# Row maxima of the scores in four row tiles of 32 rows, one group of four per key tile step

## The reference, cut to what matters

```
qh, kh, vh = proj(layernorm(x), Wq, bq), proj(ctx, Wk, bk), proj(ctx, Wv, bv)
scores = einsum('bhqd,bhkd->bhqk', qh, kh) / sqrt(16)
attn   = softmax(scores, axis=-1)          # over the 1601 keys
out    = einsum('bhqk,bhkd->bhqd', attn, vh) @ Wo.T + bo
```

## Time and profile before

| | |
|---|---|
| median of 3 runs | 684.64 us (683.98 to 685.73) |
| the profiled execution | 684.26 us, of which the profile's span is 682.4 us |
| prologue (first batch's keys and maxima) | 0 to 41 us |
| attention, 8 batches, 7 of them with units of the next | 41 to 470 us, the last batch from about 436 us |
| experts | 470 us to the end |
| busy: TensorE, VectorE, ScalarE, GpSimd | 655.0, 473.3, 326.9, 296.1 us |
| TensorE clock granted | 90% of full speed or more in all 40 slices |

### The profile page before, as it was taken

How to read it: one execution, slowest core, us unless ns; L and a number is a source line. 1 busy time by engine, 2 the same in 40 slices (tenths; PEclk the granted TensorE clock), 3 DMA queues, 4 the chain that set the end, 5 groups by cost and what they waited for, 6 DMA issues and landing times.

```text
span 682.4 us, 16188 instructions
## 1 busy us (share of the span) xinstructions
PE 655.0 (96%) x6618; PEld 538.7 (79%) x6626; DVE 473.3 (69%) x870; ACT 326.9 (48%) x533; POOL 296.1 (43%) x386
## 2 busy tenths in 40 slices
PE   7989999999999989999999999979999999999996
PEld 4778878878867867877887787656788999999996
DVE  4887757667657688584977857479778666666653
ACT  4355655554454554455446453446555444444431
POOL 1137797896676688675668766400000000000000
PEclk9999999999999999999999999999999999999999
DMA  5311110100010010011001000062003203320000
GB/s 164 144 49 51 28 48 26 49 26 26 26 35 16 26 50 25 26 34 41 9 20 48 1 2 1 2 248 88 37 1 124 103 22 124 123 109 14 0 0 31
DMA packets 12853, 34.12 MB, mean 50 GB/s; under 512 B 1515, under 2 KB 9972, under 8 KB 10612
## 3 DMA queue, kind: packets, MB, share of 16 engines
q1 hardware_dynamic: 12756, 33.19, 14.6%
q0 software_dynamic: 32, 0.01, 0.0%
HBM read 32.67 MB, written 0.52 MB: 49 GB/s over the span
## 4 chain that ended last, share of the span: by engine, by line
PE 81%; DVE 9%; issue 5%; ACT 2%; POOL 2%; DMA 0%; POOLq 0%; DVEq 0%; ACTq 0%
PE bank L1154 45%; PE bank L1340 13%; PE bank L1163 9%; PE bank L1224 5%; POOL prob_sum L481 2%; PE bank L1264 2%; PE bank L1273 2%; DVE prob_sum L481 1%; DVE ctx_lo L465 1%; DVE maxes L877 1%; ACT probs L719 1%; ACT k_hi L615 1%; PE bank L1248 1%; DVE k_lo L858 1%; PE bank L1370 1%
## 5 line engine op out<-in xcount | busy, mean ns | idle before, releaser
L481 POOL TENSOR_TENSOR prob_sum<-probs,prob_sum 128x256 f32<-128x256 f32 x336 | 266.3, 824 | 80.6 <-ACT probs L719 76.3
L719 ACT ACTIVATE probs<-bank 128x1024 f32<-128x1024 f32 (+1 forms) x104 | 106.6, 1025 | 122.9 <-PE bank L1340 107.9
L877 DVE TENSOR_REDUCE maxes<-bank 128x1 f32<-128x400 f32 (+1 forms) x256 | 131.3, 566 | 21.6 <-PE bank L1224 19.7
L701 ACT ACTIVATE h_raw<-bank,b_sb 128x512 f32<-128x512 f32 (+2 forms) x72 | 46.1, 641 | 106.5 <-PE bank L1154 106.3
L858 DVE SCALAR_TENSOR_TENSOR k_lo<-bank,bias_sb,k_hi 128x400 fp32r<-128x400 f32 (+2 forms) x64 | 40.4, 632 | 50.3 <-ACT k_hi L615 50.2
L1154 PE MATMUL bank<-w_hi,h_hi 128*128 128x256 f32 x256 | 72.7, 284 | 0.0
L1154 PE MATMUL bank<-w_hi,h_lo 128*128 128x256 f32 x256 | 72.2, 282 | 0.0
L1340 PE MATMUL bank<-qbd_hi,k_hi 64*128 64x256 f32 (+1 forms) x416 | 71.8, 339 | 0.3 <-issue 0.3
L1154 PE MATMUL bank<-w_lo,h_hi 128*128 128x256 f32 x256 | 72.1, 281 | 0.0
L1163 PE MATMUL bank<-probs,v_sb 128*32 128x128 f32 (+1 forms) x1664 | 67.0, 279 | 2.5 <-DVE masked L812 2.0
L1154 PE MATMUL bank<-wv_hi,ctx_hi 128*128 128x256 f32 (+1 forms) x208 | 65.2, 314 | 2.2 <-DVE maxes L877 1.9
(11 more groups left out here) (157 smaller groups left out, 1427.0 us busy)
## 6 DMA issues: line engine op xcount, KB each, us to landing
raw<-in_w SPq DMA_DIRECT2D x16, 1024.0 KB, 6.8
ctx_raw<-in_ctx_t SPq DMA_DIRECT2D x16, 400.0 KB, 3.7
ctx_raw<-in_ctx_t SPq DMA_DIRECT2D x8, 402.0 KB, 3.6
ctx_raw<-in_ctx_t SPq DMA_DIRECT2D x8, 399.0 KB, 3.6
w_sb<-in_w_t SPq DMA_DIRECT2D x1, 1280.0 KB
w_raw<-in_w_t SPq DMA_DIRECT2D x2, 256.0 KB, 4.6
result<-x_all SPq DMA_DIRECT2D x1, 512.0 KB, 3.0
x_all<-in_x SPq DMA_DIRECT2D x1, 384.0 KB, 4.2
```

The source lines that it names most:

```text
L481: ins = engine.tensor_tensor(prob_sum[0:ROWS[k], cols], probs[0:ROWS[k], s % 2, cols], acc[0:ROWS[k]], ALU.add)
L701: nc.scalar.activation(h_raw[:, c % 2, 0:width], bank[:, at, 0:width], ACT.Gelu, bias=b1_sb[:, bass.ds(e, 1), c:c + 1].rearrange("p a b -> ...
L719: nc.scalar.activation(probs[0:ROWS[k], s % 2, :].rearrange("p (g n) -> p g n", g=G), bank[0:ROWS[k], score_bank(b, k):score_bank(b, k) + ...
L877: nc.vector.tensor_reduce(maxes[:, g * PAIRS + j, c:c + 1], src[:, 0:width], AX.X, ALU.max).then_inc(read_dve, 1)
```

## The change

Each M unit's matmul now uses 32 rows (`MT` = 32), the 32 rows in which its two heads lie, and the four units of a K unit stand side by side in the four row tiles of 32 rows; what it computes is the same, since the other rows of the old one held zeros in these two slots. `M_AT` puts one group of four in each of steps 1 to 8, so that the group of K unit k - 1 stands in step k and step 9 has none. All four stand ahead of the step's scores. The order in `FIRST_ORDER` is the same as before; `unit_of_max` numbers the pairs of heads plainly. The scores, `denominators` and `weigh` keep their tiles.

```diff
+MT = P // PAIRS
-M_PAIRS = K_UNITS * PAIRS // ROW_TILES
-M_AT = in_order({1: 2, 2: 2, 3: 2, 4: 1, 5: 2, 6: 2, 7: 1, 8: 2, 9: 2})
+M_AT = {k: [k - 1] for k in range(1, K_UNITS + 1)}
 FIRST_ORDER = [
     [("K", 0)],
     [("K", 1)],
-    [("M", 0), ("M", 1), ("K", 2)],
+    [("M", 0), ("K", 2)],
...
-def both_tiles(pairs):
-    return [("M", ROW_TILES * u + r) for u in pairs for r in range(ROW_TILES)]
+def all_tiles(groups):
+    return [("M", PAIRS * u + j) for u in groups for j in range(PAIRS)]
...
 def step_units(k, own, following, chain):
-    m = both_tiles(M_AT.get(k, [])) if following else []
+    m = all_tiles(M_AT.get(k, [])) if following else []
...
-    ahead = len(m[:ROW_TILES])
+    ahead = len(m[:PAIRS])
...
 def unit_of_max(u):
     c, rest = divmod(u, G * PAIRS)
-    g, rest = divmod(rest, PAIRS)
-    i, r = divmod(rest, ROW_TILES)
+    g, j = divmod(rest, PAIRS)
     width = EDGE[c + 1] - EDGE[c]
-    return c, g, r * (PAIRS // ROW_TILES) + i, width + width % 2
+    return c, g, j, width + width % 2
...
                 elif kind == "M":
                     c, g, j, width = unit_of_max(u)
-                    r, i = divmod(j, PAIRS // ROW_TILES)
+                    i = j % (PAIRS // ROW_TILES)
...
-                    rows = slice(RT * r, RT * r + RT)
+                    rows = slice(MT * j, MT * j + MT)
                     ins = nc.tensor.matmul(dst[:, 0:width],
                                            qbd_hi[rows, parity, g, 2 * i:2 * i + 2, :].rearrange("p s q -> p (s q)"),
                                            k_hi[parity][rows, g, EDGE[c + 1] - width:EDGE[c + 1]],
```

More of the change, by code:

```diff
@@ L79 @@
     [("K", 1)],
[7 rows of a table removed]
+    [("M", 0), ("K", 2)],
+    [("M", 1), ("K", 3), ("V", 0)],
+    [("M", 2), ("K", 4), ("V", 1)],
+    [("M", 3), ("K", 5), ("V", 2)],
+    [("M", 4), ("K", 6), ("V", 3)],
+    [("M", 5), ("K", 7), ("V", 4)],
+    [("M", 6), ("V", 5), ("V", 6), ("M", 7)],
     [("V", 7), ("V", 8), ("V", 9), ("X", 0), ("X", 1), ("V", 10)],
@@ L254, in runs @@
     for s, units in enumerate(FIRST_ORDER):
-        row = [u for kind, n in units for u in (both_tiles([n]) if kind == "M" else [(kind, n)])]
+        row = [u for kind, n in units for u in (all_tiles([n]) if kind == "M" else [(kind, n)])]
         prologue.at[s] = [(len(order) + i, *r) for i, r in enumerate(row)]
```

## The result

After: **699.21 us** as the median of 4 runs (697.78 to 701.27), before in the same session 685.18 (683.98 to 688.52). Ratio 1.019, with an interval of 1.016 to 1.023: slower, by 13 to 14 us. The forecast was 693.1 within 684 to 699.5: the sign and most of the mechanism came out, the size was too small by 6 us. The execution that the profile shows took 701.27 us, of which the span is 699.4.

The account below looks back on a forecast made before the run. TensorE's queue was taken as the bound. Terms of 1.1 + 1.3 + 4.3 + 1.8 + 3.0 - 3.1 + 1.1 - 0.7 - 0.2 gave +8.6 us on 684.26; forecast 693.1, range 684 to 699.5.

Parts of the forecast that it names:

- the prologue's -0.2: In the prologue, only the last group of maxima is free of its wait for `k_lo`: -0.2 us.
- Four at once, and the passage: In steps with a group, four tiles cost 0.18 us and the passage from 32 to 64 rows 0.20.
- Rivals 1 and 3: At each group: 1, the passage is free, 681.6 us, chance 0.12; 3, four tiles don't run at once, 703, chance 0.07.
- Step 2's wait: At step 2's head the group waits for `k_lo` of K 1, 0.62 us in all seven batches: +4.3 us.
- Step 1's wait: At step 1's head the group waits for `k_lo` of K 0, swallowed in batch 1: +1.8 us in sum.
- Plain steps: In steps 5 to 8 the group waits 0.19 us for `k_lo` in 16 of 28 steps: +3.0 us.
- X 0: After step 9 loses its maxima, X 0 no longer waits 1.55 us for VectorE's shift in batches 4 and 6: -3.1 us.
- own work: TensorE's own work for the groups in steps 2 to 9, +0.16 us a batch: +1.1 us over seven batches.
- batch 7's self attention: In batch 7 the self attention's waits on VectorE go: -0.7 us.
- GpSimd: the step of the forecast that failed: At batch ends GpSimd's sums, with 0.98 us to spare before the denominators, limit step 9's gain: +0.35, twice.
- Rival 2: The waits on `k_lo`, 9.1 us, are swallowed because VectorE brings `k_lo` 0.6 us earlier: 684.0 us, chance 0.09.

Follow-up runs that it names:

- the tiles alone: The kernel before, its order kept, with each maxima matmul on its own 32 rows, two side by side; 706.61 us, ratio 1.030.
- half the sums: The changed kernel with GpSimd adding up only half of the probabilities in every step but a batch's first; 689.99 us, ratio 1.008.
- both edits: The changed kernel with VectorE reading step 1's maxima before the denominators and GpSimd adding up only half of the probabilities; 685.6 us, ratio 0.998.
- VectorE's maxima first: The changed kernel, but in step 1 VectorE reads the four maxima before it reads the denominators; 690.76 us, ratio 1.010.
- the group behind the scores: The changed kernel with the group of four behind the step's scores instead of ahead of them; 684.24 us, ratio 0.998.
- that kernel: The kernel before with the new order alone, all four maxima ahead of the scores, still in tiles of 64 rows; 692.5 us, ratio 1.0105.

## Why the prediction was right, and by how much it was short

For the stage the terms of the forecast sum to +8.8 (the whole sum is 8.6, with the prologue's -0.2); measured were +11.4. (684.64 and 8.6 make 693.2, where the forecast has 693.1.) Term by term:

- **Four at once, and the passage.** Priced at 0.18 and 0.20, head to K 1.54; measured 1.52 (167.44 - 165.92). Right, though the earlier trace rows did not carry the 0.20: its 0.20 runs from start to start of a matmul of 256 columns, and in a step without maxima eight pairs of such matmuls and a passage fill 1.16, some 0.12 for each pair. The 0.18 beside it, from the earlier trace rows, is free of this. Rivals 1 and 3 fall with it: the tiles alone cost 18.7 us for 105 passages, and four matmuls take the 0.45 us of two. The Trainium skill, page "TensorE: Matmul & The Clock Gate", section "Measured speedup vs the span model", gives 3.07 times for four row tiles; here four cost what a pair costs, and the measurement decides. That the estimate from this figure, about 700, lies near the measured time is chance: the time was lost elsewhere.
- **Step 2's wait.** Forecast 0.62 each; measured 0.57 (0.94 less 0.37) in all seven batches, with `k_lo` named as releaser. Right in place and nearly in size: the release was priced at 0.10 behind `k_lo` and came at 0.06 (155.76 against 155.70). Its cause was VectorE's work in step 1, as the forecast had it, though by the order of it and not the amount: with the maxima read first, steps 1 to 2 take 1.0 less.
- **Step 1's wait.** Forecast 1.8 in all. Measured head to first score, less 0.37: 0.67 in batches 1, 3, 5 and 7, 0.24 in batch 2, none in 4 and 6. Without the part of batches 5 and 7 that comes from GpSimd's lateness this is again about 1.8, but partly by luck: batch 1 has a wait that the forecast held to be swallowed, and batch 2 has 0.4 less than forecast.
- **Plain steps.** Forecast 0.19 in 16 of the 28; measured 0.15 (170.55) in 16 of the 28, 2.2 instead of 3.0. The stretch from step 2 to step 12 without X 0's relief costs +2.3 (-0.45 and 2.8), where the forecast had 3.3: 3.0 of waits, 1.0 of own work and -0.7 for batch 7's self attention.
- **X 0.** -3.1 forecast, -2.8 measured (1.39 and 1.40 in the table for batch 4, step 11 to 12, and batch 6). Right.
- **GpSimd: the step of the forecast that failed.** I found it next in line, with 0.98 us to spare, and priced it by the last sum and the denominators, +0.35 a batch. What stood first in the way was the exponential of step 0 of the next batch, which waits for the sum of two steps before, at the end of sixteen pieces without a gap. It took the whole gain of X 0 back: +1.6 in each of batches 5 and 7 from step 0 to 1, where half the sums leave 0.2. It did so by way of `k_hi`, which ScalarE makes behind that exponential and for which the group ahead of the scores waits (0.80 at 267.38). Instead of -3.1 and +0.7 the two terms came to about -2.8 and +2.8.
- **The clock: not in the sum at all.** Before has a granted clock of 1.00 over the stage, after has two falls of 3.4 us to 1.2 GHz, right behind GpSimd's waits: +1.0 and +0.8 (1.80 and 1.60 less the 0.8 of the other batches). With GpSimd's wait gone (half the sums, and both edits) no profile has a fall in the stage. With VectorE's maxima first one of the three places has it, batch 3. Before and the six kernels that have other maxima ahead of the scores have thirteen places where the exponential stands some 3.1 us for GpSimd; TensorE idles there for 0.75 to 1.20 us, and no fall follows. So falls in the stage were seen only with four tiles of 32 rows ahead of the scores and GpSimd late, and there at three places of six. What decides between the six was not isolated.
- **Outside the stage.** The prologue's +1.5 does not measure the forecast's -0.2. Before's own profile has its first score at 40.95, where four others with its prologue have it at 39.4 to 39.6; after's is at 42.43, with the clock at 1.2 GHz from 16.2 to 23.1; the group behind the scores and half the sums, with after's prologue and without this fall, have 39.6 and 39.4. This fall stands in four of the six profiles with the new prologue and in none of the seven with the old, so it is open whether it belongs to the change. The last batch's +4.1 goes with 10.2 us at 1.2 GHz. Before's profile has nothing of it, but nine of the eleven experiments' have 6.8 to 13.7 us there, the kernel before with one edit among them; this part is not the change's own. The four executions of after have a mean granted clock of 0.982 to 0.990, which is 14 to 25 us at 1.2 GHz; the profiled one has 24, and the two shortest, at 697.8, have 14, so the medians' 14.0 us is a better measure of the change than the profiles' 17.0. The runs of one kernel lie in two groups by this (before at about 684.4 and 686.9), so a difference between two single executions is uncertain by some 3 us.
- **Rival 2**, the waits swallowed: it would have taken VectorE's order of step 1 as the lever, and the run that changed this order shows that the lever exists (1.0 us a batch, 6.4 with what hangs on it). The change itself does not move it.

The stage's 2.6 us over the forecast are then +2.4 for GpSimd and X 0, +1.8 for the clock, and some -1.6 for waits and own work that came out smaller, in plain steps above all. That the total stayed within the range owes something to these signs, as they cancel in part.

What is open, besides the clock: whether GpSimd's pieces take 0.94 instead of 0.70 us at a batch's end because of what VectorE does beside them (its splits and spreads of 0.98 to 1.54 us lie there). It was read from the rows alone.

## What to carry to other kernels

Before a group of instructions is moved ahead of a critical one, ask for each of its members when its buffer comes free: the last member sets the start of all that is queued behind it, and members that run side by side leave nothing to hide its wait. Fewer streamed columns bring nothing where the narrow form pays a passage to the form of its neighbours. And when a wait goes, look not only at the next release in line but at every buffer which the next engine with little to spare still holds: here it cost as much as the wait had.

## What the runs showed of the hardware

- The passage between tiles of 32 and of 64 rows costs 0.18 to 0.20 us each, and four row tiles of 32 rows stream together in 0.45 us.
- A matmul of one tile form was seen to start beside a late one of the same form in the other row tile (x1 at 151.00, and eleven times in the stage of that kernel), but never beside a late one of the other form.
- TensorE's clock was seen at 1.2 GHz for 3.4 us at a time in the stage, for 6.8 in the prologue and for up to 10.2 in and behind the last batch, in kernels that are 96% busy. The three falls in the stage stand behind 1.0 to 1.4 us in which TensorE had waited, and last while it is busy: 3.40 of 3.40 us at 268.8. At three more places with the same waits it did not fall.
